# An attention stage reordered: next step's first scores beside this step's second scores, output product ahead of the gates

## The chip, the cores and the metric

The kernel runs on one core of a Trainium2 chip. Its time is the device time of one launch in microseconds; the number given is the median of several runs.

## What is computed

Sixteen sequences of 256 tokens with 256 features pass through a mixture-of-experts layer, an attention layer with 16 heads, the experts again, and a closing part (look-up-table FFN, gated recurrence, FFN). The change touches the attention layer alone. Cut to what matters:

```
q = x @ Wq ; k = x @ Wk ; v = x @ Wv ; s = clip(x @ Ws, -32, 32)      # x: normalised stream, per head 64, 64, 128, 64 wide
z = cumlogsumexp(s) ; p = exp(s - z) ; g = exp(z[t-1] - z[t])          # 64 slots a head
hk[t] = hk[t-1] * g[t] + k[t] p[t]^T ; ok[t] = q[t] @ hk[t]            # first read: a score for each slot
pv = softmax(ok)
hv[t] = hv[t-1] * g[t] + p[t] v[t]^T ; ov[t] = pv[t] @ hv[t]           # second read: over the slots
o = rmsnorm(ov) * g_norm * silu(x @ Wg) ; out = x + o @ Wo
```

The kernel has no recurrence. Since `p` and `g` are ratios of running sums of exp(s), the first read is a causal product (scores q k^T, masked, times exp(s), divided by the running sum), and the second is another (scores of the divided softmax weights with exp(s), masked, times v).

## The kernel before

`attention` (from line 803) works in N = 64 steps: 16 sequences of 4 quads of heads (HQ = 4, QPB = 4), T = 256 tokens as TT = 2 tiles of 128, heads in NH = 2 pairs. Each engine has a list of its own written out by hand; semaphores (`wait_ge`, `then_inc`) tie them. An engine runs its list strictly in order, so a wait holds all that stands behind it. Step n works on quad n while projections and first scores of quad n+1 are made ahead.

TensorE's list in a step is the loop at the end of the function: `value(n+1,0)`, `slots_read(n)` (first read: masked scores `at` times exps, into bank psC[0], semaphore `ok_ps`), `state_of_slots(n)` (sum over the first tile, psB[0]), `slots(n+1)` (projection for s), `turn_back(n)` (transposes of `okn`, the divided first read; waits `okn_ok`), `value(n+1,1)`, `query(n+1)`, `turn_weights(n)`, `turn_exps(n+1)`, `turn_output(n-1)`, `key(n+1)`, `scores_b(n)` (second scores, own 128x128 blocks only, psB), `state_read(n)` (psD), `gate(n+1,0)`, every fourth step `turn_stream`, `gate(n+1,1)`, `over_j(n)` (masked second scores times v, psD), `output(n-1)` (product with Wo, psC[0]) and `scores_a(n+1)` (first scores, four heads, each in a bank of its own: a 256-column and a 128-column matmul). The contraction of scores and state reads is 64 rows, so heads of the two parities stand in different halves of the array. Projections and `output` split each factor in a high and a low part and take three products (`split_matmul`, lines 1488 to 1490).

VectorE (DVE) in a step: `okn(n)` (line 1170), `clip(n+1)`, maximum, subtraction and sum of the softmax, `pzT` (1188), `low_of_output(n-1)`, `masked_second(n)` (1123), `running_sum` twice (1140), `invert` twice (reciprocal, 1144), `gated_output(n,1)` and `(n,0)` (1133), `gate(n+1,0)` and `(n+1,1)` (1129), `add_output(n-1)` (1107), `masked_first(n+1)` (1117, four parts of 384 columns), `squares(n)` (1148, 1151). ScalarE (ACT) copies out of PSUM (line 989), takes exp (1011, 1052), the squares (1067) and the gate's tanh (1027), in the order of its own loop. GpSimd (POOL) makes the root of the norm (978), scales the output (983) and, between, a table look-up.

PSUM has eight banks: psA and psB and psC two each, psD two. Reuse of a bank is what many waits are for.

Of the kernel before, what the change touches and what calls it, by code (L numbers as in the profile page):

```python
# [21 lines left out]
P = 128  # L22
# [780 lines left out]
def attention(nc, cst, w, tag, past, stream_a, stream_b, x_out, second, zero_row, indices, looked_up):  # L803
# [10 lines left out]
    with ExitStack() as ctx:  # L814
# [16 lines left out]
        at = mem.sb("at", [P, HQ, 3 * P])  # L831
        bt = at.rearrange("p h i -> p (h i)")[:, 0:HQ * T].rearrange("p (q s i) -> p q s i", q=2, i=P)
        state = at.rearrange("p h i -> p (h i)")[:, HQ * T:HQ * T + NH * DV].rearrange("p (a v) -> p a v", a=NH)
        sq = mem.sb("sq", [P, TT * HQ * DV])
        okn = sq[:, 0:NH * T].rearrange("p (a t) -> p a t", a=NH)
# [18 lines left out]
        psO = [psD[:, k, :] for k in range(2)]  # L854
        first_banks = psB + [psC[1], psO[0]]
# [4 lines left out]
                 "at_ps at_ok ok_ps st_ps st_ok okn_ok okb_ps mx_ok sub_ok pe_ok sm_ok es_ok ezt_ps pzt_ok bt_ps bt_ok "  # L860
# [4 lines left out]
         at_ps, at_ok, ok_ps, st_ps, st_ok, okn_ok, okb_ps, mx_ok, sub_ok, pe_ok, sm_ok, es_ok, ezt_ps, pzt_ok, bt_ps, bt_ok,  # L865
# [21 lines left out]
        with nc.Block(no_gpsimd_drain=True) as block:  # L887
# [99 lines left out]
            def _(act):  # L987
# [3 lines left out]
                def high_of_stream(b):  # L991
                    act.wait_ge(ln_ps, b + 1)
                    if b > 0:
                        act.wait_ge(g_ps, TT * QPB * b)
                    copy(lnT[:, 0, :, :].rearrange("p c t -> p (c t)"), psC[0], lnTh_ok)
# [26 lines left out]

                def gate_tanh(m, t):
                    if m > 0:
                        act.wait_ge(o1_ok, TT * m)
                    act.wait_ge(g_ps, TT * m + t + 1)
                    nc.scalar.activation(tg[:, t, :], psA[(1 - m % 2) if t == 0 else m % 2], ACT.Tanh, scale=0.5).then_inc(th_ok, 1)
# [11 lines left out]
                key(0)  # L1039
                turned_exps(0)  # L1040
                gate_tanh(0, 0)
                gate_tanh(0, 1)
                for n in range(N):
# [13 lines left out]
                    if ahead:  # L1057
                        key(n + 1)
                        turned_exps(n + 1)
                        if (n + 1) % QPB == QPB - 1 and n + 2 < N:  # L1060
                            high_of_stream((n + 1) // QPB + 1)
                    for p in range(2):
                        if p == 0:
                            act.wait_ge(ov_ps, 2 * n + 1)
# [3 lines left out]
                    if ahead:  # L1068
                        gate_tanh(n + 1, 0)
                        gate_tanh(n + 1, 1)  # L1070
                high_of_output(N - 1)

            @block.vector
            def _(dve):
# [14 lines left out]
                def low_of_stream(b):  # L1089
                    dve.wait_ge(lnTh_ok, b + 1)  # L1090
                    nc.vector.tensor_tensor(out=lnT[:, 1, :, :].rearrange("p c t -> p (c t)"), in0=psC[0],
# [21 lines left out]

                def masked_first(m):
                    for h in range(HQ):
                        dve.wait_ge(at_ps, HQ * m + h + 1)
                        nc.vector.tensor_tensor(out=at[:, h, :], in0=first_banks[h][:, 0:3 * P],
                                                in1=cst["causal"][:, :, :].rearrange("p a i -> p (a i)"), op=ALU.mult).then_inc(at_ok, 1)

                def masked_second(n):  # L1120
                    for p in range(2):
                        dve.wait_ge(bt_ps, 2 * n + p + 1)
                        nc.vector.tensor_tensor(out=bt[:, p, :, :], in0=psB[p].rearrange("p (s i) -> p s i", i=P),  # L1123
                                                in1=cst["causal"][:, 0, :].unsqueeze(1).to_broadcast([P, HQ, P]), op=ALU.mult).then_inc(bt_ok, 1)
# [35 lines left out]
                for a in range(NH):  # L1160
                    invert(0, a)
                gate(0, 0)
                gate(0, 1)
                masked_first(0)
                for n in range(N):
# [26 lines left out]
                    if ahead:  # L1192
                        dve.wait_ge(pzt_ok, n + 1)
                        running_sum(n + 1, 0)
                        running_sum(n + 1, 1)
                        invert(n + 1, 0)
                        if (n + 1) % QPB == QPB - 1 and n + 2 < N:
                            low_of_stream((n + 1) // QPB + 1)
                        invert(n + 1, 1)
                    dve.wait_ge(ov_ps, 2 * n + 2)  # L1200
# [7 lines left out]
                    if n > 0:  # L1208
                        add_output(n - 1)
                    if ahead:  # L1210
                        masked_first(n + 1)
# [5 lines left out]
            def _(pe):  # L1217
                ident = cst["ident"][:, :]

                def turn_stream(b):  # L1220
                    pe.wait_ge(ln_ok, TT * b + TT)
                    if b > 0:
                        pe.wait_ge(pzt_ok, QPB * b - 1)
                    for t in range(TT):
                        for c in range(DC):
                            mm = nc.tensor.transpose(psC[0][:, c * T + t * P:c * T + (t + 1) * P], ln[:, t, c * P:(c + 1) * P], ident)
# [45 lines left out]
                def gate(m, t):  # L1272
                    if t == 0:
                        pe.wait_ge(q_ok, m + 1)
                    else:
                        pe.wait_ge(k_ok, m + 1)
# [8 lines left out]

                def scores_a(m):
# [830 lines left out]
```

## Time and profile before

| | us |
|---|---|
| median of 3 runs | 2667.67 (2666.32 to 2668.74) |
| the profiled execution's own time | 2663.76 |
| its span, first to last instruction | 2662.0 |
| TensorE matmul busy | 2339.8 |
| VectorE busy | 1749.2 |
| ScalarE busy | 887.0 |
| GpSimd busy | 1238.2 |

The page cuts the span into 40 slices of 66.6 us; its digits are tenths of a slice that an engine was busy, or of full speed that TensorE's clock was granted. Attention takes the slices from about the sixth to the 27th. Busy times of overlapping matmuls are not their cost: that is read from start to start. "Idle before" behind an instruction is how long its engine stood, with what released it.

### The profile page before, as it was taken

What the parts mean: (1) busy time and instruction counts of PE and PEld (TensorE: products, weight loads), DVE (VectorE), ACT (ScalarE), POOL (GpSimd) and SP (SyncE); (2) the same over time, 40 slices, a digit from 0 to 9 for tenths busy, and PEclk for the clock granted to TensorE, in tenths of its full rate; (3) what the DMA queues carried; (4) which work ended last, traced back from release to release, by engine and by line L of the source; (5) the groups of instructions that cost most, each with busy time, mean ns of one, the idle gap of its engine ahead of it and who ended that gap; (6) DMA issues with size and microseconds to landing.
All of it is one profiled execution on the core that took longest, in us unless ns stands there. A gap on an engine that the chain in (4) does not pass through costs nothing. (4 is left out here: it accounts for less than half of the span.)

```text
span 2662.0 us, 45792 instructions
## 1 busy us (share of the span) xinstructions
PE 2339.8 (88%) x17782; PEld 2078.3 (78%) x17782; DVE 1749.2 (66%) x3450; ACT 887.0 (33%) x1768; POOL 1238.2 (47%) x1214
## 2 busy tenths in 40 slices
PE   7556499999999999999999999987566489999998
PEld 6444379999999999999999999976455377888887
DVE  6433267877787778777877887766422266776654
ACT  4323233333333333333333333324322133333332
POOL 3377735555555555545554555452378512222111
PEclk9698999999999999999999999998698798999999
DMA  7999700000000000000000000006699600000000
GB/s 241 291 222 225 145 13 9 17 17 21 5 21 17 21 5 17 21 21 5 17 21 21 6 17 21 13 3 175 178 231 215 137 20 21 25 24 25 14 12 16
DMA packets 196934, 169.60 MB, mean 64 GB/s; under 512 B 28945, under 2 KB 189681, under 8 KB 196209
## 3 DMA queue, kind: packets, MB, share of 16 engines
q1 hardware_dynamic: 168144, 123.94, 15.6%
q0 software_dynamic: 24576, 37.77, 7.8%
q10 hardware_dynamic: 4000, 4.98, 0.6%
q8 instruction: 143, 2.34, 0.4%
q14 instruction: 71, 0.57, 0.1%
HBM read 117.94 MB, written 53.13 MB: 64 GB/s over the span
## 5 line engine op out<-in xcount | busy, mean ns | idle before, releaser
L978 POOL TENSOR_TENSOR a_orstd<-a_ms,minus_half 128x8 f32<-128x8 f32 x64 | 106.7, 1667 | 466.3 <-DVE a_ms L1151 466.3
L958 POOL TENSOR_SCALAR a_pick<-a_index,lut_row 128x258 f32<-128x258 int32 x240 | 280.8, 1170 | 24.3
L1144 DVE RECIPROCAL a_rz<-a_rz 128x256 f32<-128x256 f32 x128 | 215.6, 1716 | 0.0
L777 DVE TENSOR_TENSOR e_hT<-e_psH,e_sil 128x128 f32<-128x128 f32 x128 | 37.2, 291 | 263.2 <-ACT e_sil L735 263.1
L661 PE MATMUL e_psX<-ident,e_xg 128*128 128x128 f32 x256 | 61.1, 325 | 166.8 <-DMA e_xg<-rows,slot_tok 166.6
L661 PEld LDWEIGHTS e_psX<-ident,e_xg 128*128 128x128 f32 x256 | 31.6, 156 | 209.7 <-DMA e_xg<-rows,slot_tok 205.4
L961 POOL TENSOR_TENSOR a_found<-a_found,a_pick 128x258 f32<-128x258 f32 x240 | 177.2, 738 | 20.0
L631 POOL DMA_INDIRECT e_xg<-rows,slot_tok x128 | 128.3, 1002 | 108.2 <-POOLq L253 69.8
L989 ACT ACTIVATE a_v<-a_psA 128x512 f32<-128x512 f32 x128 | 76.6, 598 | 229.5 <-PE a_psA L1490 229.5
L1488 PE MATMUL a_psC<-wo_high,a_oT 128*128 128x256 f32 x512 | 150.5, 294 | 1.5 <-DVE a_oT L1097 1.5
L1488 PE MATMUL f_pair<-f_lnT,wguT 128*128 128x512 f32 (+1 forms) x352 | 143.5, 408 | 7.5 <-DVE f_lnT L1754 7.2
L1489 PE MATMUL a_psC<-wo_low,a_oT 128*128 128x256 f32 x512 | 144.7, 283 | 0.0
L1490 PE MATMUL a_psC<-wo_high,a_oT 128*128 128x256 f32 x512 | 144.7, 283 | 0.0
L1765 DVE TENSOR_TENSOR f_hs<-f_pair,f_sil 128x512 f32<-128x512 f32 x96 | 66.0, 689 | 116.7 <-PE f_pair L1490 106.5
L1490 PE MATMUL f_pair<-f_lnT,wguT 128*128 128x512 f32 (+1 forms) x352 | 140.8, 400 | 0.0
L1489 PE MATMUL f_pair<-f_lnT,wguT 128*128 128x512 f32 (+1 forms) x352 | 140.7, 400 | 0.0
L983 POOL TENSOR_TENSOR a_o<-a_o,a_orstd 128x512 f32<-128x512 f32 x128 | 131.0, 1044 | 5.0
L1067 ACT ACTIVATE a_sq<-a_psD 128x512 f32<-128x512 f32 x128 | 76.5, 598 | 164.2 <-DVE a_o L1133 98.1
L1371 PEld LDWEIGHTS a_psD<-a_v,a_at 128*128 128x128 f32 x1024 | 124.1, 191 | 5.7
L1662 ACT ACTIVATE f_sil<-f_pair 128x512 f32<-128x512 f32 x96 | 57.2, 597 | 210.6 <-PE f_pair L1490 210.6
L719 ACT ACTIVATE e_xgT<-e_psX 128x256 f32<-128x256 f32 x128 | 49.1, 383 | 229.9 <-PE e_psX L661 225.8
L1123 DVE TENSOR_TENSOR a_at<-a_psB,causal 128x512 f32<-128x512 f32 x128 | 82.4, 686 | 64.5 <-PE a_psB L1320 64.5
(263 smaller groups left out, 7825.8 us busy)
## 6 DMA issues: line engine op xcount, KB each, us to landing
e_wg<-in_L_ffn_w_gate SPq DMA_DIRECT2D x128, 128.0 KB, 3.3
e_wu<-in_L_ffn_w_up SPq DMA_DIRECT2D x128, 128.0 KB, 3.7
e_wd<-in_L_ffn_w_down SPq DMA_DIRECT2D x128, 128.0 KB, 4.1
rows<-r_row SPq DMA_DIRECT2D x32, 320.0 KB, 3.3
stream_b<-r_zeros SPq DMA_DIRECT2D x11, 384.0 KB
stream_c<-rows SPq DMA_DIRECT2D x33, 128.0 KB, 3.2
r_xt<-in_L_attn_hidden_states SPq DMA_DIRECT2D x16, 256.0 KB, 5.8
stream_a<-r_xt SPq DMA_DIRECT2D x16, 256.0 KB, 4.3
```

The source lines that it names most:

```text
L631: pool.indirect_dma_start(out=xg[:, e % U, :], out_offset=None, in_=rows, in_offset=bass.IndirectOffsetOnAxis(ap=slot_tok[:, e:e + 1], axi ...
L661: nc.tensor.transpose(psX[u][:, c, :], xg[:, e % U, c * P:(c + 1) * P], cst["ident"][:, :]).then_inc(turned[u], 1)
L958: nc.gpsimd.tensor_scalar(pick[:, :, :], index[:, :, :], float(c), w["lut"][:, c:c + 1], ALU.is_equal, ALU.mult).then_inc(picked, 1)
L961: nc.gpsimd.tensor_tensor(out=found[:, :, :], in0=found[:, :, :], in1=pick[:, :, :], op=ALU.add).then_inc(looked, 1)
L978: nc.gpsimd.tensor_tensor(out=flat(orstd[:, :, :]), in0=ms[:, :], in1=cst["minus_half"][:, 0:TT * HQ], op=ALU.pow).then_inc(orstd_ok, 1)
L983: nc.gpsimd.tensor_tensor(out=part, in0=part, in1=orstd[:, :, 2 * a:2 * a + 2].unsqueeze(3).to_broadcast([P, TT, 2, DV]), op=ALU.mult).the ...
L1123: nc.vector.tensor_tensor(out=bt[:, p, :, :], in0=psB[p].rearrange("p (s i) -> p s i", i=P), in1=cst["causal"][:, 0, :].unsqueeze(1).to_br ...
L1144: nc.vector.reciprocal(rz[:, a, :], rz[:, a, :]).then_inc(rz_ok, 1)
L1371: mm = nc.tensor.matmul(psD[:, p, (t * NH + a) * DV:(t * NH + a + 1) * DV], bt[:, p, a * TT + t, :], v[:, n % 2, t, h * DV:(h + 1) * DV], ...
L1488: nc.tensor.matmul(out, lhs[0], rhs[0], start=first, stop=False)
L1489: nc.tensor.matmul(out, lhs[0], rhs[1], start=False, stop=False)
L1490: return nc.tensor.matmul(out, lhs[1], rhs[0], start=False, stop=last)
```

## The change

The first scores lose their own banks and shape. `own_scores` now makes the 128x128 diagonal blocks of either score product (first or second), two banks with four blocks each: for the first scores in psA, for the second in psB as before. The lower blocks (queries of the second tile, keys of the first) go by `scores_below` to the first half of psD's two banks, which ACT copies to a new tile `below` without a mask. DVE masks the diagonal blocks in two operations (`masked`) instead of four.

In TensorE's list `scores_a(n+1)` and `scores_below(n+1)` stand between `scores_b(n)` and `state_read(n)`; `output(n-1)` and `over_j(n)` follow, and then the gates, which now wait for the masks (`at_ok`), since they reuse psA. `value(n+1,0)` stands behind `state_of_slots(n)`. `over_j` waits for `below_ok` and signals once (`ov_ps`) instead of per parity. In DVE's list `masked_first(n+1)` follows `masked_second(n)`, `add_output(n-1)` is ahead of the gated outputs, and the two `invert` and `low_of_stream` are behind the gates, ahead of `squares(n)`. In ACT's list `below_copy` is ahead of `turned_exps`, and `high_of_stream` behind the tanhs. `turn_stream` uses psB[1] instead of psC[0]. `bt` moves from the tile of `at` into that of `sq`.

```diff
--- before.py
+++ after.py
...
@@ -1019,6 +1018,11 @@
                 def state_copy(n):
                     act.wait_ge(st_ps, n + 1)
                     copy(flat(state), psS, st_ok)
+
+                def below_copy(m):
+                    act.wait_ge(below_ps, m + 1)
+                    for p in range(2):
+                        copy(flat(below[:, p, :, :]), psD[:, p, 0:NH * P], below_ok)
 
                 def gate_tanh(m, t):
                     if m > 0:
@@ -1037,6 +1041,7 @@
                 value(0, 1)
                 query(0)
                 key(0)
+                below_copy(0)
                 turned_exps(0)
                 gate_tanh(0, 0)
                 gate_tanh(0, 1)
@@ -1056,18 +1061,19 @@
                         high_of_output(n - 1)
                     if ahead:
                         key(n + 1)
+                        below_copy(n + 1)
                         turned_exps(n + 1)
-                        if (n + 1) % QPB == QPB - 1 and n + 2 < N:
-                            high_of_stream((n + 1) // QPB + 1)
                     for p in range(2):
                         if p == 0:
-                            act.wait_ge(ov_ps, 2 * n + 1)
+                            act.wait_ge(ov_ps, n + 1)
                         else:
                             act.wait_ge(o1_ok, 2 * n + 1)
                         nc.scalar.activation(of_parity(p, sq), read_out(p), ACT.Square).then_inc(sq_ok, 1)
                     if ahead:
                         gate_tanh(n + 1, 0)
                         gate_tanh(n + 1, 1)
+                        if (n + 1) % QPB == QPB - 1 and n + 2 < N:
+                            high_of_stream((n + 1) // QPB + 1)
                 high_of_output(N - 1)
 
             @block.vector
...
@@ -1111,17 +1117,17 @@
                     dve.wait_ge(s_ps, m + 1)
                     nc.vector.tensor_scalar(flat(em[:, :, :]), psA[1 - m % 2], -32.0, 32.0, ALU.max, ALU.min).then_inc(sc_ok, 1)
 
+                def masked(out, banks, at, ready, done):
+                    for p in range(2):
+                        dve.wait_ge(ready, 2 * at + p + 1)
+                        nc.vector.tensor_tensor(out=out[:, p, :, :], in0=banks[p].rearrange("p (s i) -> p s i", i=P),
+                                                in1=cst["causal"][:, 0, :].unsqueeze(1).to_broadcast([P, HQ, P]), op=ALU.mult).then_inc(done, 1)
+
                 def masked_first(m):
-                    for h in range(HQ):
-                        dve.wait_ge(at_ps, HQ * m + h + 1)
-                        nc.vector.tensor_tensor(out=at[:, h, :], in0=first_banks[h][:, 0:3 * P],
-                                                in1=cst["causal"][:, :, :].rearrange("p a i -> p (a i)"), op=ALU.mult).then_inc(at_ok, 1)
+                    masked(at, [psA[1 - m % 2], psA[m % 2]], m, at_ps, at_ok)
 
                 def masked_second(n):
-                    for p in range(2):
-                        dve.wait_ge(bt_ps, 2 * n + p + 1)
-                        nc.vector.tensor_tensor(out=bt[:, p, :, :], in0=psB[p].rearrange("p (s i) -> p s i", i=P),
-                                                in1=cst["causal"][:, 0, :].unsqueeze(1).to_broadcast([P, HQ, P]), op=ALU.mult).then_inc(bt_ok, 1)
+                    masked(bt, psB, n, bt_ps, bt_ok)
 
                 def gate(m, t):
 
@@ -1159,9 +1165,9 @@
                     running_sum(0, a)
                 for a in range(NH):
                     invert(0, a)
+                masked_first(0)
                 gate(0, 0)
                 gate(0, 1)
-                masked_first(0)
                 for n in range(N):
                     b, q = divmod(n, QPB)
                     ahead = n + 1 < N
@@ -1190,14 +1196,13 @@
                         low_of_output(n - 1)
                     masked_second(n)
                     if ahead:
+                        masked_first(n + 1)
                         dve.wait_ge(pzt_ok, n + 1)
                         running_sum(n + 1, 0)
                         running_sum(n + 1, 1)
-                        invert(n + 1, 0)
-                        if (n + 1) % QPB == QPB - 1 and n + 2 < N:
-                            low_of_stream((n + 1) // QPB + 1)
-                        invert(n + 1, 1)
-                    dve.wait_ge(ov_ps, 2 * n + 2)
+                    if n > 0:
+                        add_output(n - 1)
+                    dve.wait_ge(ov_ps, n + 1)
                     dve.wait_ge(tg_ok, TT * n + TT)
                     gated_output(n, 1)
                     dve.wait_ge(sq_ok, 2 * n + 1)
@@ -1205,10 +1210,10 @@
                     if ahead:
                         gate(n + 1, 0)
                         gate(n + 1, 1)
-                    if n > 0:
-                        add_output(n - 1)
-                    if ahead:
-                        masked_first(n + 1)
+                        if (n + 1) % QPB == QPB - 1 and n + 2 < N:
+                            low_of_stream((n + 1) // QPB + 1)
+                        invert(n + 1, 0)
+                        invert(n + 1, 1)
                     squares(n)
                 low_of_output(N - 1)
                 add_output(N - 1)
@@ -1220,10 +1225,10 @@
                 def turn_stream(b):
                     pe.wait_ge(ln_ok, TT * b + TT)
                     if b > 0:
-                        pe.wait_ge(pzt_ok, QPB * b - 1)
+                        pe.wait_ge(bt_ok, 2 * (QPB * b - 1))
                     for t in range(TT):
                         for c in range(DC):
-                            mm = nc.tensor.transpose(psC[0][:, c * T + t * P:c * T + (t + 1) * P], ln[:, t, c * P:(c + 1) * P], ident)
+                            mm = nc.tensor.transpose(psB[1][:, c * T + t * P:c * T + (t + 1) * P], ln[:, t, c * P:(c + 1) * P], ident)
                     mm.then_inc(ln_ps, 1)
 
                 def project(name, dst, m, t, width, ready):
@@ -1270,10 +1275,7 @@
                     project_turned("k", psA[m % 2], m, k_ps)
 
                 def gate(m, t):
-                    if t == 0:
-                        pe.wait_ge(q_ok, m + 1)
-                    else:
-                        pe.wait_ge(k_ok, m + 1)
+                    pe.wait_ge(at_ok, 2 * m + t + 1)
                     project("g", psA[(1 - m % 2) if t == 0 else m % 2], m, t, HQ * DV, g_ps)
 
                 def turn_exps(m):
@@ -1283,21 +1285,33 @@
                             mm = nc.tensor.transpose(psC[1][:, a * T + t * P:a * T + (t + 1) * P], em[:, t, a * P:(a + 1) * P], ident)
                     mm.then_inc(et_ps, 1)
 
+                def own_scores(lhs, rhs, banks, ready):
+
+                    for a in range(NH):
+                        for t in range(TT):
+                            for p in range(2):
+                                r, own = p * DK, slice(t * P, (t + 1) * P)
+                                mm = nc.tensor.matmul(banks[p][:, (a * TT + t) * P:(a * TT + t + 1) * P], lhs[r:r + DK, a, own], rhs[r:r + DK, a, own],
+                                                      start=True, stop=True)
+                                if a == NH - 1 and t == TT - 1:
+                                    mm.then_inc(ready, 1)
+
                 def scores_a(m):
 
                     pe.wait_ge(k_ok, m + 1)
                     pe.wait_ge(q_ok, m + 1)
-                    pe.wait_ge(et_ok, m + 1)
-                    if m > 0:
-                        pe.wait_ge(bt_ok, 2 * m)
-                    for h in range(HQ):
-                        if h == 3 and m > 0:
-                            pe.wait_ge(o1_ok, TT * m)
-                            pe.wait_ge(sq_ok, TT * m)
-                        bank, a, r = first_banks[h], h // 2, (h % 2) * DK
-                        nc.tensor.matmul(bank[:, 0:2 * P], kT[r:r + DK, a, 0:P], qT[r:r + DK, a, 0:T], start=True, stop=True)
-                        nc.tensor.matmul(bank[:, 2 * P:3 * P], kT[r:r + DK, a, P:T], qT[r:r + DK, a, P:T],
-                                         start=True, stop=True).then_inc(at_ps, 1)
+                    own_scores(kT, qT, [psA[1 - m % 2], psA[m % 2]], at_ps)
+
+                def scores_below(m):
+
+                    if m > 1:
+                        pe.wait_ge(otl_ok, NH * (m - 1))
+                    for a in range(NH):
+                        for p in range(2):
+                            r = p * DK
+                            mm = nc.tensor.matmul(psD[:, p, a * P:(a + 1) * P], kT[r:r + DK, a, 0:P], qT[r:r + DK, a, P:T], start=True, stop=True)
+                    if m == 0:
+                        mm.then_inc(below_ps, 1)
 
                 def state_of_slots(n):
 
@@ -1313,36 +1327,34 @@
                     pe.wait_ge(pzt_ok, n + 1)
                     pe.wait_ge(et_ok, n + 1)
                     pe.wait_ge(st_ok, n + 1)
-                    for a in range(NH):
-                        for t in range(TT):
-                            for p in range(2):
-                                r, own = p * M, slice(t * P, (t + 1) * P)
-                                mm = nc.tensor.matmul(psB[p][:, (a * TT + t) * P:(a * TT + t + 1) * P], emT[r:r + M, a, own], pzT[r:r + M, a, own],
-                                                      start=True, stop=True)
-                                if a == NH - 1 and t == TT - 1:
-                                    mm.then_inc(bt_ps, 1)
-
-                def state_read(n):
+                    pe.wait_ge(lnTl_ok, n // QPB + 1)
+                    own_scores(emT, pzT, psB, bt_ps)
+
+                def state_read(n, more):
 
                     if n > 0:
                         pe.wait_ge(otl_ok, NH * n)
                     for a in range(NH):
                         for p in range(2):
                             r = p * M
-                            nc.tensor.matmul(psD[:, p, (NH + a) * DV:(NH + a + 1) * DV], pzT[r:r + M, a, P:T], state[r:r + M, a, :],
-                                             start=(a == 0), stop=False, skip_group_check=True)
+                            mm = nc.tensor.matmul(psD[:, p, (NH + a) * DV:(NH + a + 1) * DV], pzT[r:r + M, a, P:T], state[r:r + M, a, :],
+                                                  start=(a == 0), stop=False, skip_group_check=True)
+                    if more:
+                        mm.then_inc(below_ps, 1)
 
                 def slots_read(n):
 
                     if n > 1:
                         pe.wait_ge(acc_ok, n - 1)
+                    pe.wait_ge(at_ok, 2 * n + 2)
+                    pe.wait_ge(below_ok, 2 * n + 2)
                     for a in range(NH):
-                        pe.wait_ge(at_ok, HQ * n + 2 * a + 2)
-                        for i, (t, j) in enumerate(((0, 0), (1, 0), (1, 1))):
-                            for h in (2 * a, 2 * a + 1):
-                                r = (h % 2) * M
+                        for t, j in ((0, 0), (1, 0), (1, 1)):
+                            for p in range(2):
+                                h, r = 2 * a + p, p * M
+                                scores = at[:, p, a * TT + t, :] if t == j else below[:, p, a, :]
                                 mm = nc.tensor.matmul(psC[0][r:r + M, a * T + t * P:a * T + (t + 1) * P], em[:, j, h * M:(h + 1) * M],
-                                                      at[:, h, i * P:(i + 1) * P], start=(j == 0), stop=(j == t))
+                                                      scores, start=(j == 0), stop=(j == t))
                     mm.then_inc(ok_ps, 1)
 
                 def turn_back(n):
@@ -1363,6 +1375,8 @@
 
                 def over_j(n):
 
+                    if n + 1 < N:
+                        pe.wait_ge(below_ok, 2 * n + 4)
                     for p in range(2):
                         pe.wait_ge(bt_ok, 2 * n + p + 1)
                         for a in range(NH):
@@ -1370,7 +1384,7 @@
                                 h = 2 * a + p
                                 mm = nc.tensor.matmul(psD[:, p, (t * NH + a) * DV:(t * NH + a + 1) * DV], bt[:, p, a * TT + t, :],
                                                       v[:, n % 2, t, h * DV:(h + 1) * DV], start=False, stop=True, skip_group_check=True)
-                        mm.then_inc(ov_ps, 1)
+                    mm.then_inc(ov_ps, 1)
 
                 def turn_output(n):
                     for a in range(NH):
@@ -1397,16 +1411,16 @@
                 query(0)
                 key(0)
                 turn_exps(0)
+                scores_a(0)
+                scores_below(0)
                 gate(0, 0)
                 gate(0, 1)
-                scores_a(0)
                 for n in range(N):
                     ahead = n + 1 < N
-                    if ahead:
-                        value(n + 1, 0)
                     slots_read(n)
                     state_of_slots(n)
                     if ahead:
+                        value(n + 1, 0)
                         slots(n + 1)
                     turn_back(n)
                     if ahead:
@@ -1420,18 +1434,18 @@
                     if ahead:
                         key(n + 1)
                     scores_b(n)
-                    state_read(n)
+                    if ahead:
+                        scores_a(n + 1)
+                        scores_below(n + 1)
+                    state_read(n, ahead)
+                    if n > 0:
+                        output(n - 1)
+                    over_j(n)
                     if ahead:
                         gate(n + 1, 0)
                         if (n + 1) % QPB == QPB - 1 and n + 2 < N:
                             turn_stream((n + 1) // QPB + 1)
                         gate(n + 1, 1)
-                    over_j(n)
-                    if n > 0:
-                        pe.wait_ge(lnTl_ok, min((n + 1) // QPB + (2 if (n + 1) % QPB == QPB - 1 else 1), B))
-                        output(n - 1)
-                    if ahead:
-                        scores_a(n + 1)
                 turn_output(N - 1)
                 pe.wait_ge(acc_ok, N - 1)
                 output(N - 1)
```

## Rows read from the trace of the kernel before

**Rows 1.** the page, section 2: 40 slices of the span

```profile
PE   7556499999999999999999999987566489999998
PEclk9698999999999999999999999998698798999999
```

**Rows 2.** stretches (begin:end, length, busy PE, PEld, DVE, ACT, POOL, clock, DMA)

```profile
1002.44:1024.77 22.33, 22.33 (x193) 20.25 (x192) 18.09 (x31) 7.89 (x15) 14.14 (x15) 1.00 0.15 48
```

**Rows 3.** timeline of PE, one step (start, us, engine, line, out<-in, count)

```profile
1002.24 0.28 PE L1490 MATMUL a_psC<-wo_high,a_oT 128*128 128x256 f32 x1
1002.45 0.71 PE L1298 MATMUL a_psB<-a_qT,a_kT 64*128 64x256 f32 x4
1004.05 0.50 PE L1488 MATMUL a_psA<-wv_high,a_lnT 128*128 128x512 f32 x1
...
1005.32 0.39 PE L1490 MATMUL a_psA<-wv_high,a_lnT 128*128 128x512 f32 x1
1005.64 1.53 PE L1344 MATMUL a_psC<-a_at,a_em 128*64 128x128 f32 x24
...
1007.54 0.39 PE L1488 MATMUL a_psA<-ws_high,a_lnT 128*128 128x256 f32 x1
...
1008.96 0.28 PE L1490 MATMUL a_psA<-ws_high,a_lnT 128*128 128x256 f32 x1
1009.08 0.38 PE L1353 MATMUL a_psC<-ident,a_sq 128*128 128x128 f32 x2
```

**Rows 4.** timeline of PE, later in this step

```profile
1015.61 1.16 PE L1320 MATMUL a_psB<-a_pzT,a_emT 64*128 64x128 f32 x16
1016.60 0.61 PE L1332 MATMUL a_psD<-a_at,a_pzT 64*128 64x128 f32 x8
...
1019.81 0.39 PE L1490 MATMUL a_psA<-wg_high,a_lnT 128*128 128x512 f32 x1
```

**Rows 5.** timeline of DVE, around this step

```profile
1001.99 1.28 DVE L1129 SCALAR_TENSOR_TENSOR a_tg<-a_tg,a_psA 128x512 f32<-128x512 f32 x2 [0.67 <-ACT a_tg L1027]
1003.19 0.68 DVE L1107 TENSOR_TENSOR a_xacc<-a_psC,a_xacc 128x512 f32<-128x512 f32 x1
...
1019.17 3.34 DVE L1144 RECIPROCAL a_rz<-a_rz 128x256 f32<-128x256 f32 x2
1022.43 1.22 DVE L1133 TENSOR_TENSOR a_o<-a_psD,a_tg 128x512 f32<-128x512 f32 x2
```

**Rows 6.** timelines of PE (10.68) and ACT, in this step

```profile
1010.68 0.39 PE L1490 MATMUL a_psA<-wv_high,a_lnT 128*128 128x512 f32 x1
...
1001.36 1.09 ACT L1027 ACTIVATE a_tg<-a_psA 128x512 f32<-128x512 f32 x2
...
1011.11 0.60 ACT L989 ACTIVATE a_v<-a_psA 128x512 f32<-128x512 f32 x1 [0.48 <-PE a_psA L1490]
...
1015.71 0.60 ACT L989 ACTIVATE a_kT<-a_psA 128x512 f32<-128x512 f32 x1 [0.78 <-PE a_psA L1490]
```

**Rows 7.** timelines of DVE and PE, last step

```profile
1770.40 1.21 DVE L1148 TENSOR_REDUCE a_ss<-a_sq 128x8 f32<-128x1024 f32 x1
...
1771.73 0.69 DVE L1170 TENSOR_TENSOR a_sq<-a_psC,a_rz 128x512 f32<-128x512 f32 x1
1772.47 0.66 PE L1353 MATMUL a_psC<-ident,a_sq 128*128 128x128 f32 x4 [0.62 <-DVE a_sq L1170]
```

**Rows 8.** timeline of PE in the expert stages, two waits

```profile
263.47 0.44 PE L661 MATMUL e_psX<-ident,e_xg 128*128 128x128 f32 x2 [2.47 <-DMA e_xg<-rows,slot_tok]
...
1960.68 0.44 PE L661 MATMUL e_psX<-ident,e_xg 128*128 128x128 f32 x2 [2.28 <-DMA e_xg<-rows,slot_tok]
```

**Rows 9.** stretches and PE's waits in the expert stages

```profile
262.00:316.00 54.00, 30.27 (x204) 23.41 (x204) 18.53 (x39) 14.98 (x37) 43.35 (x33) 1.00 0.81 176
1961.30:1964.70 3.40, 3.40 (x17) 3.11 (x16) 0.77 (x2) 1.27 (x4) 2.79 (x3) 0.51 0.66 144
PE e_psX L661 <- DMA e_xg<-rows,slot_tok: 24.0, 16, 2.5
```

More of the change, by code:

```diff
@@ L830, in attention @@
         rz = mem.sb("rz", [P, NH, T])
-        at = mem.sb("at", [P, HQ, 3 * P])
-        bt = at.rearrange("p h i -> p (h i)")[:, 0:HQ * T].rearrange("p (q s i) -> p q s i", q=2, i=P)
-        state = at.rearrange("p h i -> p (h i)")[:, HQ * T:HQ * T + NH * DV].rearrange("p (a v) -> p a v", a=NH)
+        at = mem.sb("at", [P, 2, HQ, P])
+        below = mem.sb("below", [P, 2, NH, P])
+        state = below[:, 0, :, :]
         sq = mem.sb("sq", [P, TT * HQ * DV])
+        bt = sq.rearrange("p (q s i) -> p q s i", q=2, i=P)
         okn = sq[:, 0:NH * T].rearrange("p (a t) -> p a t", a=NH)
@@ L853, in attention @@
         psD = mem.ps("psD", [P, 2, 512])
-        psO = [psD[:, k, :] for k in range(2)]
-        first_banks = psB + [psC[1], psO[0]]
         psS = psB[0][:, 0:NH * DV]
@@ L859, in attention @@
                  "v_ps v_ok q_ps q_ok k_ps k_ok g_ps th_ok tg_ok s_ps sc_ok em_ok scan_ok rz_ok et_ps et_ok "
-                 "at_ps at_ok ok_ps st_ps st_ok okn_ok okb_ps mx_ok sub_ok pe_ok sm_ok es_ok ezt_ps pzt_ok bt_ps bt_ok "
+                 "at_ps at_ok below_ps below_ok ok_ps st_ps st_ok okn_ok okb_ps mx_ok sub_ok pe_ok sm_ok es_ok ezt_ps pzt_ok bt_ps bt_ok "
                  "ov_ps sq_ok ss_ok ms_ok orstd_ok o1_ok o2_ok ot_ps oth_ok otl_ok out_ps acc_ok "
@@ L864, in attention @@
          v_ps, v_ok, q_ps, q_ok, k_ps, k_ok, g_ps, th_ok, tg_ok, s_ps, sc_ok, em_ok, scan_ok, rz_ok, et_ps, et_ok,
-         at_ps, at_ok, ok_ps, st_ps, st_ok, okn_ok, okb_ps, mx_ok, sub_ok, pe_ok, sm_ok, es_ok, ezt_ps, pzt_ok, bt_ps, bt_ok,
+         at_ps, at_ok, below_ps, below_ok, ok_ps, st_ps, st_ok, okn_ok, okb_ps, mx_ok, sub_ok, pe_ok, sm_ok, es_ok, ezt_ps, pzt_ok, bt_ps, bt_ok,
          ov_ps, sq_ok, ss_ok, ms_ok, orstd_ok, o1_ok, o2_ok, ot_ps, oth_ok, otl_ok, out_ps, acc_ok,
@@ L994, in high_of_stream @@
                         act.wait_ge(g_ps, TT * QPB * b)
-                    copy(lnT[:, 0, :, :].rearrange("p c t -> p (c t)"), psC[0], lnTh_ok)
+                    copy(lnT[:, 0, :, :].rearrange("p c t -> p (c t)"), psB[1], lnTh_ok)
                 def value(m, t):
@@ L1090, in low_of_stream @@
                     dve.wait_ge(lnTh_ok, b + 1)
-                    nc.vector.tensor_tensor(out=lnT[:, 1, :, :].rearrange("p c t -> p (c t)"), in0=psC[0],
+                    nc.vector.tensor_tensor(out=lnT[:, 1, :, :].rearrange("p c t -> p (c t)"), in0=psB[1],
                                             in1=lnT[:, 0, :, :].rearrange("p c t -> p (c t)"), op=ALU.subtract).then_inc(lnTl_ok, 1)
```

## The prediction

> **What bounds the kernel now.** I read the page's slices first: TensorE is at 99% with a full clock from about 340 to 1770 us, the attention stage, and nothing outside that stage is touched by the change [rows 1]. Then one stretch: in a step of 22.33 us PE is busy throughout, VectorE (DVE) for 18.1, ScalarE (ACT) for 7.9 [rows 2]. A busy PE may still be waiting with overlapped ends, so I read PE's timeline next, by the starts of its matmuls. One step of the 64 takes 22.33 us (it begins with `scores_a` at 1002.45, the next at 1024.77 [rows 2, 3]), and every section follows the one before at 0.09 to 0.2 us above its normal spacing. PE is the bound, with no wait that costs more than a change of shape. DVE is idle for 4.2 us of the step [rows 2]. So the change can win only by making PE's list shorter, and loses where a new order makes PE wait for the slack engine. I therefore cost first the list, then each wait.
>
> **PE's own list.** Starts, not durations, are added here, since matmuls overlap.
> - Removed: the shape change after the output product (2.24 to 2.45 against a spacing of 0.12: 0.09), `scores_a` alone (2.45 to 4.05: 1.60), `value(n+1,0)` after it (4.05 to 5.64: 1.59), `slots` as the first 128-row section after `state_of_slots` (7.54 to 9.08: 1.54) [rows 3]. Sum 4.82.
> - Added: own and lower blocks as 12 pairs of 64-row matmuls, 2 passes each. `scores_b` has the same form: 16 passes in 8 pairs take 0.99 with the start-up, and the 8 passes of `state_read` go on behind it [rows 4]; that is 0.109 a pair once started, so 12 x 0.109 = 1.31 with no start-up, between `scores_b` and `state_read`. `slots_read` behind the gates costs 0.32 from the last matmul (5.32 to 5.64 [rows 3]) in place of the plain spacing of a 512-column matmul, 0.23 (4.05 to 5.32 is five of them and 0.1 of start-up): 0.09. `value(n+1,0)` now starts the 128-row section: 6 x 0.233 + 0.11 = 1.51. `slots` behind it has no start-up (7.54 to 8.96 is eleven spacings and 0.11, so 0.119 each): 12 x 0.118 = 1.42. Sum 4.33.
> - So PE's list falls by 0.49, from 22.33 to 21.84 us. Over the 63 steps that make a next one: -31 us. `output` and `over_j` change places with the gates at no cost: the same kinds of neighbours.
>
> Here a rule speaks against the change. The Trainium skill, "TensorE: Matmul & The Clock Gate", section "LDWEIGHTS (loading the stationary operand)", says that a weight load takes its columns at 1.2 GHz, so about 107 ns for 128. The blocks need 24 loads where 16 stood; were the 8 more not hidden, they would cost an estimated 0.85 us a step, 54 us in all, and PE's list would grow by 0.36. I go by the row of `scores_b`, where 16 such loads fit into 0.99 us.
>
> **Edits with no price.** DVE masks two whole banks in place of four parts (two 128x512 operations, about 0.6 apart as the gates are [rows 5]) right behind the second mask; the gates' new wait for it is met while PE still has `output` and `over_j` to do. The two `below_copy` on ACT stand between `state_read` and `over_j`, with `output` (24 x 0.12 = 2.9 us) as cover; two copies at most as long as a 512-column one are 1.2 [rows 6], and without the cover `over_j` would wait that long. `scores_a` needs the copied keys: the key copy runs from 15.71 to 16.31 [rows 6], and `scores_b` ends at 16.60 [rows 4], so it is there 0.3 early; bounds are 0 and 0.3, I take 0 by these rows. `add_output` and the single `ov_ps` add no lateness: both are ahead of the gates. The moved `turn_stream` costs PE the same; SP's queue and POOL's list have no step moved.
>
> **The wait that is added.** Behind the gates, DVE now does gate 0, gate 1, both `invert`, `squares(n)`, and only then `okn(n+1)`, the product that `turn_back(n+1)` on PE waits for. Before, the two inversions ran under the gates' matmuls, and PE had `over_j`, `output`, `scores_a` and `value` to do meanwhile. Both sides of the race, from the start of the last gate matmul:
> - DVE's side. The `tanh` starts 0.43 behind the last 512-column matmul (the value copy: 10.68 to 11.11 [rows 6]). Gate 1 starts 0.63 after its tanh (1001.36 to 1001.99 [rows 5, 6]); the inversions start 0.61 later (half of 1.99 to 3.19), and the two take 3.26 (19.17 to 22.43) [rows 5]. `squares` to `okn` takes 1.33, and `okn` to the first matmul of `turn_back` 0.74: the last step already shows this, since DVE is late there, and PE stands 0.62 us for it [rows 7]. Sum 0.43 + 0.63 + 0.61 + 3.26 + 1.33 + 0.74 = 7.00 us.
> - PE's side, without waiting: 0.32 to `slots_read`, 1.90 for it and `state_of_slots` (5.64 to 7.54 [rows 3]), 1.51, 1.42: 5.15 us.
> - So `turn_back` waits 1.85 us, in every step from 1 to 63. Everything behind it on PE (`value(n+1,1)`, query, weights, key, scores, output, `over_j`, gates) is in the same queue, and the next race starts only when the gates end, so nothing catches up. The period is 21.84 + 1.85 = 23.69. DVE's other idle time lies in front of `add_output` and of the gated outputs, ahead of the gates, where it helps nothing.
> The term has bounds of 1.55 and 2.15 (0.05 less or more at each of six hand-overs, an estimate from one of them: 0.63 from start to start, 0.67 by its idle time [rows 5]). I take 1.85, the sum of the rows.
>
> In 15 steps a stream is turned between the gates, and its `low_of_stream` now stands ahead of the inversions: 0.6 us more each, 9 us. At the end `output(62)` no longer covers the tail of `over_j(63)`: about 3 us.
>
> **The clock.** A step gets an idle stretch on PE of 1.85 less 0.16 of the last matmul's tail, 1.7 us, and about 2.3 in the 15. After an idle stretch of 2.28 us the granted clock was 0.51 for the next 3.4 us; after one of 2.47 it stayed full, and in 54 us with 16 waits of 1.5 on average (24.0 in all) it stayed 1.00 [rows 8, 9]. I take none for the 1.7 and half of the 15, 7 x 1.7 (half of 3.4 us of work lost) = 12 us.
>
> **Sum.** -31 + 63 x 1.85 (117) + 9 + 3 + 12 = +110 us. Against the profiled execution's own 2663.8 us this is 2774; the median of the runs shown stands 3.9 us above it, so 2778.
>
> **Rivals.**
> - The low clock spreads (12%). If the stall is rather 2.15 or more, many of the 63 are followed by a low stretch at 1.7 to 3.4 us each: -31 + 135 + 9 + 3, and 25 x 2.2 = 55: +171, 2839. For it: the 2.28 us row [rows 8]. Against: the 16 waits of 1.5, of which the longest was 2.5.
> - DVE keeps up and the kernel is faster (8%). DVE is idle for 4.2 us of a step [rows 2], and masks less than before. If the chain behind the gates were at most 5.15 us, `turn_back` would find `okn` done: only -31 + 3 + 0 is left, 2640. It decides at a chain of 5.15; for that the inversions would have to run ahead of gate 1. The order in DVE's list forbids it, and the last step shows that `okn` really stands behind `squares`.
> - In between (7%): a chain of 5.6 to 6.4 us, a stall of 0.5 to 1.2, and with it 2681 to 2725.
> - The 8 additional loads are not hidden (3%). Each would then cost at most one more spacing of a pair, 0.109 [rows 4]: 0.87 us a step, 55 in all, 2833. The section of the Trainium skill named above bears on this.
> - The likeliest (70%): 2778, alone from 2747 to 2809 by the bounds of the stall and of the clock.
>
> Range: 2738 to 2832 leaves out the faster rival, half of the low-clock one and some of the middle. A difference under 0.2% (5 us) is about what a measurement of this kernel can't tell from none. Faster by more: 8%; within: 2%; slower: 90%.
>
> **What the profile after would show.** PE: an idle stretch of 1.7 us ahead of `turn_back` in each step, put down to DVE's `a_sq` product, with no `over_j` or score wait. DVE: no idle time from gate 1 to `okn`, the inversions behind the gates; idle ahead of `add_output` and the gated outputs. A period near 23.7 us. Twelve score pairs at 0.109 between `scores_b` and `state_read`. The prediction is wrong if `turn_back` follows `slots` at once, if `scores_a` waits for the key copy, if `over_j` waits for ACT's copies, or if the clock's row shows falls in the attention stage beyond a few.

## The result and the profile after

| | before | after |
|---|---|---|
| median of 4 runs, us | 2666.99 | 2777.66 (2775.72 to 2780.87) |
| ratio, 95% interval | | 1.0416 (1.0404 to 1.0429) |
| profiled execution, span | 2662.0 | 2774.7 |
| attention, first to last matmul | 1462.2 | 1571.0 |
| a plain step, `turn_back` to `turn_back`, median | 22.33 | 23.77 |

The changed kernel is 4.2% slower. Of the 112.7 us in the span, 108.8 lie between the first and the last attention matmul, and 3.9 outside. A plain step is one without the turned stream between its gates; the 15 with it are called stream steps below. The page's slices (now 69.4 us each), which answer to [rows 1], look alike: attention is as full and its clock digits are as high, so the loss is not to be seen in this view:

```profile
PE   6556489999999999999999999996566568999998
PEclk9688899999999999999999999997789979999999
```

One step as a stretch (columns as in [rows 2]). PE, busy for all of 22.33 us before, is now idle for 1.7 of 23.80, while VectorE is busy for 16.9:

```profile
1020.21:1044.01 23.80, 22.09 (x204) 20.10 (x202) 16.89 (x24) 8.55 (x16) 10.06 (x10) 1.00 0.06 12
```

TensorE in this step, which answers to [rows 3, 4]. The gate's last matmul is at 1029.40, `value` follows `state_of_slots` at 1031.63, and after the last of `slots` (1034.45) the engine stands until 1036.43. Below, `scores_b`, the own blocks, the lower blocks and `state_read` run in one go, the 24 passes of the new scores from 1044.01 to 1045.35:

```profile
1029.40 0.40 PE L1504 MATMUL a_psA<-wg_high,a_lnT 128*128 128x512 f32 x1
1029.73 0.44 PE L1356 MATMUL a_psC<-a_at,a_em 128*64 128x128 f32 x4
...
1031.63 0.50 PE L1502 MATMUL a_psA<-wv_high,a_lnT 128*128 128x512 f32 x1
...
1034.45 0.28 PE L1504 MATMUL a_psA<-ws_high,a_lnT 128*128 128x256 f32 x1
1036.43 0.66 PE L1365 MATMUL a_psC<-ident,a_sq 128*128 128x128 f32 x4 [1.70 <-DVE a_sq L1176]
...
1043.01 1.16 PE L1294 MATMUL a_psB<-a_pzT,a_emT 64*128 64x128 f32 x16
1044.01 1.06 PE L1294 MATMUL a_psA<-a_qT,a_kT 64*128 64x128 f32 x16
1044.90 0.61 PE L1312 MATMUL a_psD<-a_qT,a_kT 64*128 64x128 f32 x8
1045.35 0.61 PE L1340 MATMUL a_psD<-a_below,a_pzT 64*128 64x128 f32 x8
1045.89 0.39 PE L1502 MATMUL a_psC<-wo_high,a_oT 128*128 128x256 f32 x1
```

ScalarE's second tanh and VectorE behind the gates, which answer to [rows 5 to 7]. No gap is left between gate 1 and the product `a_sq<-a_psC,a_rz` (that is `okn`), which ends the wait:

```profile
1029.89 0.60 ACT L1031 ACTIVATE a_tg<-a_psA 128x512 f32<-128x512 f32 x1 [0.80 <-PE a_psA L1504]
```

```profile
1030.53 0.69 DVE L1135 SCALAR_TENSOR_TENSOR a_tg<-a_tg,a_psA 128x512 f32<-128x512 f32 x1 [0.71 <-ACT a_tg L1031]
1031.13 3.36 DVE L1150 RECIPROCAL a_rz<-a_rz 128x256 f32<-128x256 f32 x2
1034.40 1.16 DVE L1154 TENSOR_REDUCE a_ss<-a_sq 128x8 f32<-128x1024 f32 x1
...
1035.68 0.69 DVE L1176 TENSOR_TENSOR a_sq<-a_psC,a_rz 128x512 f32<-128x512 f32 x1
```

TensorE's largest wait in attention, from 400 to 1800 us (total, times, longest):

```profile
PE a_psC L1365 <- DVE a_sq L1176: 104.5, 58, 2.1
```

One wait for the masks is there too, once, before the first step. There no `output` and no `over_j` stand between the scores and the first gate, and on VectorE the masks stand behind both inversions, so TensorE is idle for 3.30 us:

```profile
349.90 3.34 DVE L1150 RECIPROCAL a_rz<-a_rz 128x256 f32<-128x256 f32 x2
353.16 1.22 DVE L1123 TENSOR_TENSOR a_at<-a_psA,causal 128x512 f32<-128x512 f32 x2
```

```profile
353.84 0.79 PE L1502 MATMUL a_psA<-wg_high,a_lnT 128*128 128x512 f32 x1 [3.30 <-DVE a_at L1123]
```

### The profile page after: what moved, and what is told of

It is laid out like the page before. It is cut to its first block and busy times, and to the rows that moved or that the text cites. A ratio compares the mean times of both kernels' runs of the same rounds, so it can differ in the third digit from the quotient of the medians.

```text
span 2774.7 us, 46756 instructions
## 1 busy us (share of the span) xinstructions
PE 2331.5 (84%) x18294; PEld 2072.2 (75%) x18294; DVE 1730.7 (62%) x3322; ACT 927.9 (33%) x1896; POOL 1237.2 (45%) x1214
## 5 line engine op out<-in xcount | busy, mean ns | idle before, releaser
L1135 DVE SCALAR_TENSOR_TENSOR a_tg<-a_tg,a_psA 128x512 f32<-128x512 f32 x128 | 88.0, 687 | 104.1 <-ACT a_tg L1031 104.1
L1365 PE MATMUL a_psC<-ident,a_sq 128*128 128x128 f32 x256 | 42.4, 289 | 116.0 <-DVE a_sq L1176 116.0
L1139 DVE TENSOR_TENSOR a_o<-a_psD,a_tg 128x512 f32<-128x512 f32 x128 | 84.7, 691 | 69.8 <-PE a_psD L1385 69.8
```

The costliest lines, as they stand in the source:

```text
L1135: nc.vector.scalar_tensor_tensor(out=tg[:, t, :], in0=tg[:, t, :], scalar=1.0, in1=psA[(1 - m % 2) if t == 0 else m % 2], op0=ALU.add, op1 ...
L1139: nc.vector.tensor_tensor(out=of_parity(p, flat(o1[:, :, :])), in0=read_out(p), in1=of_parity(p, flat(tg[:, :, :])), op=ALU.mult).then_inc ...
```

## Experiments

All times are medians; the ratio is to the kernel before, run beside it on the same chip (e1, e2, e4 and e7 on one chip, e3, e5 and e6 on another, e8 and e9 on a third). "Period" is the median from one `turn_back` to the next; "gap" is the time from the start of the matmul ahead of `turn_back` to its own, 0.12 us where nothing is waited for. A row that begins with PEld counts the idle time of the weight loads, which is somewhat longer than the delay from start to start. The theory was that the time is lost in a race behind the gates: VectorE's chain up to `okn` against the TensorE work up to `turn_back`. Such a race has a bend: as long as VectorE's side is the shorter one, its length costs nothing; beyond that, each microsecond costs one.

**e1_inverts_ahead.**

```diff
                         running_sum(n + 1, 1)
+                        invert(n + 1, 0)
+                        invert(n + 1, 1)
                     if n > 0:
                         add_output(n - 1)
...
                         gate(n + 1, 1)
...
-                        invert(n + 1, 0)
-                        invert(n + 1, 1)
```

> The changed kernel with one edit in VectorE's list: both inversions stand right behind the running sums, ahead of the output addition, instead of behind the gates. Theory (the wait is a race behind the gates): the chain from the last gate matmul to the first matmul of turn_back falls from 7.03 to 3.8 us, against 5.2 us of TensorE work; no wait at turn_back, a period of 21.9 us, about 2644 us. Rival 1 (the new score blocks and the new order on TensorE cost the time themselves): the period stays near 23.8 and the time within 10 us of 2778. Rival 2 (the inversions are only moved to another late place: VectorE comes 0.9 us late to the gated outputs, and tanh, gates and squares pass it on): a wait of 0.9 us stays, about 2700.

2644.4 us, ratio 0.9911 (0.9895 to 0.9928), period 21.87. The whole loss goes, and a gain stays. VectorE is in fact late for the output addition and the gated outputs, but both end in time:

```profile
1012.46 3.34 DVE L1150 RECIPROCAL a_rz<-a_rz 128x256 f32<-128x256 f32 x2
1015.72 0.63 DVE L1113 TENSOR_TENSOR a_xacc<-a_psC,a_xacc 128x512 f32<-128x512 f32 x1
1016.26 1.28 DVE L1139 TENSOR_TENSOR a_o<-a_psD,a_tg 128x512 f32<-128x512 f32 x2
1018.20 1.49 DVE L1135 SCALAR_TENSOR_TENSOR a_tg<-a_tg,a_psA 128x512 f32<-128x512 f32 x2 [0.67 <-ACT a_tg L1031]
1019.61 1.21 DVE L1154 TENSOR_REDUCE a_ss<-a_sq 128x8 f32<-128x1024 f32 x1
...
1020.94 0.68 DVE L1176 TENSOR_TENSOR a_sq<-a_psC,a_rz 128x512 f32<-128x512 f32 x1
```

`okn` would allow `turn_back` from 1021.68, and TensorE comes to it at 1023.04, at its plain spacing:

```profile
1022.93 0.28 PE L1504 MATMUL a_psA<-ws_high,a_lnT 128*128 128x256 f32 x1
1023.04 0.49 PE L1365 MATMUL a_psC<-ident,a_sq 128*128 128x128 f32 x3
```

Both rivals fall: the new order on TensorE costs nothing by itself, and VectorE's lateness is not passed on. This is also the fastest kernel of the study, 0.9% ahead of the one before and 4.8% ahead of the changed one.

**e2_one_ahead.** Only `invert(n + 1, 0)` is moved ahead.

> The changed kernel with one of the two inversions moved ahead of the output addition, the other left behind the gates. Theory: the chain is 7.03 less 1.65 = 5.4 us against 5.2, so 0.2 us of wait is left and all but a tenth of it is gone: about 2656. Rival (each inversion takes its own share, half of the wait stays): 0.93 us a step, about 2710.

2670.4 us, ratio 1.0009 (0.9997 to 1.0021), period 22.18. The direction and the bend are the theory's: of 1.86 us of wait 0.25 is left, not half. The size was missed by 14 us, in my own count. The plain steps lose 0.3 to e1 and not 0.2; the 15 stream steps lose 0.62 each (23.19 against 22.57), because `low_of_stream` stands behind the gates too, and I had left them out; the last interval and the tail behind it are 2.6 longer together. The wait and the one for the turned stream, from 400 to 1700 us:

```profile
PEld a_psC L1365 <- DVE a_sq L1176: 22.8, 58, 0.7
...
PEld a_psA L1502 <- DVE a_lnT L1097: 6.2, 15, 0.4
```

**e3_one_between.** One inversion ahead, the other between the two gates.

> The changed kernel with one inversion ahead of the output addition and the other between the two gates, where VectorE stands 1.15 us for the second tanh. Theory: the chain from the last gate matmul is 0.5 us of gate 1's delay longer than with both ahead, still under 5.2: no wait at turn_back, the time of e1_inverts_ahead within 3 us, and low_of_stream keeps its place. Rival (the second gate's delay is passed on whole, 1.65 us): a wait of 0.3 us, 20 us above e1_inverts_ahead.

2651.3 us, ratio 0.9937 (0.9916 to 0.9957), period 21.87 as in e1: no wait at `turn_back`. It is 7 us over e1 and not within 3, though part of that may lie between two chips: between the first and the last attention matmul the traces differ by 5.0. These are not where the rival had them either, in each step, but in the 15 stream steps (22.92 against 22.57): the delayed gate delays `low_of_stream`, and `value` of the next sequence waits for it, 0.77 us a time against 0.41 in e1. First e3, then e1:

```profile
PEld a_psA L1502 <- DVE a_lnT L1097: 11.5, 15, 0.8
```

```profile
PEld a_psA L1502 <- DVE a_lnT L1097: 6.2, 15, 0.4
```

**e7_half_sum.** The sum of squares reads half of each head's values, so half of the norm's sum is left out.

```diff
-                    nc.vector.reduce_sum(ss[:, :], sq.rearrange("p (s v) -> p s v", v=DV), axis=AX.X).then_inc(ss_ok, 1)
+                    nc.vector.reduce_sum(ss[:, :], sq.rearrange("p (s v) -> p s v", v=DV)[:, :, 0:DV // 2], axis=AX.X).then_inc(ss_ok, 1)
```

> The changed kernel, its sum of squares taken over half of each head's 128 values: the reduction reads 512 columns instead of 1024, and half of the norm's sum is left out. Nothing is moved. Theory (all that VectorE does behind the gates is in the race): the chain is 0.5 us shorter, the wait 1.35 instead of 1.86, 33 us less, and a few low clock stretches less: about 2742. Rival (only the inversions count, since the squares have slack of their own): 2778.

2739.2 us, ratio 1.0265 (1.0247 to 1.0282), period 23.26. The gap before `turn_back` falls from 1.98 to 1.44 us, which is 34 us in all, and the four low-clock stretches of the changed kernel's stream steps are gone, some 6 more; 38 were measured. What is saved in an operation that was not moved comes off the wait in full too: the race is over everything behind the gates, not over the inversions. TensorE's wait from 400 to 1700 us:

```profile
PE a_psC L1365 <- DVE a_sq L1176: 69.7, 55, 1.5
```

**e4_extra_op.** One idle operation more behind the inversions.

```diff
...
+                        if n > 0:
+                            dve.wait_ge(idled, n)
+                        nc.vector.reduce_max(idle[:, :], cst["causal"][:, :, :], axis=AX.X).then_inc(idled, 1)
                     squares(n)
```

> The changed kernel with one more VectorE operation behind the inversions in each step, a maximum over 384 constant columns, some 0.4 us, whose result nothing reads. Theory: the wait grows by the operation's whole duration, 0.4 x 63 = 26 us, to 2804; idle stretches of 2.1 us on TensorE in plain steps are then as long as the ones of the 15 stream steps are now, of which 5 were followed by a low clock, so about a third of the 63 steps is followed by one, 16 more at 1.55 us: 25 us, about 2829. Rival (the low clock needs a longer idle stretch than that and came by another cause): 2804 with no more low stretches than now.

2834.0 us, ratio 1.0619 (1.0602 to 1.0637). The gap before `turn_back` is 2.43 us, 0.45 longer, and a plain step 24.25; that is 28 us of the 56 over the changed kernel. The rest is the clock. In the attention stage it fell 22 times next to a `turn_back`, against 5 times in the changed kernel, and a step with such a fall is 1.55 us longer: 17 more are 26 us. Clock digits of the page, and the wait from 400 to 1700 us:

```profile
PEclk9788799999999999999999999997878979999999
```

```profile
PE a_psC L1369 <- DVE a_sq L1177: 116.7, 52, 2.5
```

**e5_scores_alone.** The new blocks between `scores_b` and `state_read`; gates, `over_j` and `output` in the order of before; `value(n+1,0)` ahead of `slots_read`; on VectorE the inversions (with `low_of_stream` between them) behind the running sums, and the output addition behind the gates.

> The scores' part of the change alone: own and lower blocks between scores_b and state_read, but gates, over_j and output in the order of the kernel before, value ahead of slots_read, and VectorE's inversions ahead of the gated outputs, as before. Theory (the new blocks save 0.42 us of TensorE's list a step, as the changed kernel's period of 23.77 less 1.86 of wait shows; the gates now wait about 0.3 us for the masks, which four operations of 0.6 us behind scores_b give): a period of 22.2, about 2660. Rival (the 8 more weight loads eat the gain): at least 2667, with scores_b and the blocks at more than 0.12 us a pair.

2689.4 us, ratio 1.0079 (1.0062 to 1.0096), period 22.37. Slower than I expected by 29 us, though not by the rival's mechanism: the pairs run at 0.11 us. Read from the waits, the blocks' saving is spent on VectorE. The first gate stands for the masked product in each step (first line): it starts 0.46 us behind the last of `state_read`, against 0.20 in the kernel before, so 0.26 late. `value(n+1,0)` starts another 0.17 late behind `output` (0.29 against 0.12); in its list it waits for the first gate's product, though the profile names no releaser (second line). The saving without the neighbouring `value` and `slots` is 0.09 + 1.60 - 1.31 = 0.38, so 22.33 - 0.38 + 0.26 + 0.17 = 22.38 for a plain step, which is even with before. In the stream steps, 23.9 us against 23.0, `value` of the next sequence stands 1.1 us for the gate (third line), which I read as the gate and the turned stream standing behind four masks on VectorE; no run takes that apart. The lead-in adds 4 us, with the 3.3 us wait for the first masks that the changed kernel has too:

```profile
PEld a_psA L1503 <- DVE a_at L1123: 21.5, 57, 0.4
```

```profile
1019.99 0.19 PEld L1503 LDWEIGHTS a_psA<-wv_high,a_lnT 128*128 128x128 f32 x1 [0.18 <-issue]
```

```profile
PE a_psA L1503 <- DVE a_tg L1135: 15.4, 14, 1.4
```

**e6_over_j_first.** e1 with `over_j` ahead of `output`, and `add_output` behind the gated outputs.

> Kernel e1_inverts_ahead with over_j ahead of output on TensorE, and the output addition behind the gated outputs on VectorE. Theory (output is the cover of ACT's two copies and of the second mask): over_j waits about 0.9 us in each step, so 57 us above e1: about 2700. Rival (the copies and masks are early anyway): the time of e1, 2644.

2694.4 us, ratio 1.0094 (1.0075 to 1.0114), period 22.75, 0.87 above e1, as the theory had it: without `output` as cover, `over_j` stands for ACT's copies of the lower blocks, in 57 steps of 57:

```profile
PEld a_psD L1385 <- ACT a_below L988: 54.1, 57, 0.9
```

**e8_slack_two and e9_slack_five.** e1 with two and with five of the idle operations behind the gates, for the bend of the race.

> Kernel e1_inverts_ahead with two of e4's idle VectorE operations (0.45 us each from start to start) behind the gates. In e1's trace okn would let turn_back start at 1021.68 (1020.94 and 0.74) and it starts at 1023.05: 1.37 us of slack. Theory (a race with a bend): 0.9 us more stays under the slack, so plain steps cost nothing, and the 15 stream steps, where 0.6 of slack is used already, at most 0.15 each: the time of e1, 2644, within 4 us. Rival (the wait is proportional to what VectorE does behind the gates, with no bend): 0.9 x 63 = 57 us more, 2701.

2648.3 us, ratio 0.9921 (0.9904 to 0.9938): two are free, as e1's slack of 1.37 us says.

> Kernel e1_inverts_ahead with five of the idle operations, 2.25 us, behind the gates. Theory: 2.25 less 1.37 of slack is 0.88 us of wait in the plain steps and about 0.5 more in the 15 stream steps: 55 + 7 us above e1, about 2706. Rival (no bend): 2.25 x 63 = 142 us more, 2786.

2750.3 us, ratio 1.0304 (1.0286 to 1.0322), dearer than I expected by 44 us. The price of the operations was wrong, not the bend. In a row each waits for the one before, and the five take 2.81 us (16.52 to 19.33), not 2.25: they start 0.58 to 0.59 apart, and only behind the last, which nothing waits for, is it 0.47. 2.81 - 1.37 = 1.44 is just the wait that the trace has (a gap of 1.56 less the spacing of 0.12):

```profile
1016.52 2.90 DVE L1221 TENSOR_REDUCE a_idle<-causal 128x3 f32<-128x384 f32 x5
1019.33 1.21 DVE L1155 TENSOR_REDUCE a_ss<-a_sq 128x8 f32<-128x1024 f32 x1
```

```profile
PE a_psC L1370 <- DVE a_sq L1177: 76.3, 55, 1.6
```

## Why the prediction was right, point by point

The time came 0.3 us from the forecast. Its mechanism is shown; the last few microseconds of closeness are luck, since small terms missed both ways. In the profiled executions the change is 112.7 us where 110 were forecast: -29 from PE's list (forecast -31), 117 of wait (117), 3 of slower transposes (0), 5 in the stream steps (9), 6 of clock (12), 7 at the ends (3) and 4 outside the attention matmuls (0). The forecast then added 3.9 us to get from the profiled execution to the median; for the changed kernel this was 1.2.

- **PE's own list.** Forecast 21.84 us a step. e1, which has no wait, measures 21.87; the 8 more weight loads are hidden, as the row of `scores_b` had said: the 12 new pairs take 1.34 us (1044.01 to 1045.35), 0.112 each, where 1.31 was forecast. The rival of unhidden loads falls.
- **The race.** Chain forecast 7.00, measured 7.03 (1029.40 to 1036.43): tanh after 0.49, gate 1 after 0.64, inversions after 0.60, 3.27 for the two, 1.28 from `squares` to `okn`, 0.75 to `turn_back`. PE's side forecast 5.15, measured 5.17 (1029.40 to 1034.45, and 0.12). Wait 1.86 against 1.85. e1, e2, e7 and e9 move either side by known amounts and the wait follows.
- **A plain step.** Forecast 23.69, measured 23.77, 5 us in all. PE's list has 0.03 of it, and after a wait the four transposes of `turn_back` take 0.41 from their start to the next section's, against 0.35 in a running stream (all of e1, e3, e6 and the kernel before). The forecast had nothing for that.
- **The stream steps.** I put 0.6 on each for `low_of_stream`; they lose 1.77 (23.03 to 24.80) where a plain step loses 1.44 (22.33 to 23.77), so 0.33 more, because in them `value` already stands 0.24 for the turned stream, and that part of TensorE's list overlaps the longer chain. 5 us instead of 9.
- **The clock.** Forecast 7 falls in the 15, with idle stretches of about 2.3 us, and 12 us; the stretches measure 2.05, and 4 of the 15 were followed by a fall: 6 us. One more fall came at the last `turn_back`, so "5 of the 15" in what was expected of e4 is one too many. The rival of a spreading low clock, told by a stall of 2.15 or more, is just what e4 brings about with a stall of 2.31 (a gap of 2.43 less 0.12).
- **The ends.** Forecast 3. The lead-in to the first `turn_back` is 3.7 longer, the last interval 2.8 (a plain one 1.4), the tail 2.0: about 7 instead of 3. The lead-in is where an edit with no price had one: I had the gates' new wait for the masks met while PE does `output` and `over_j`, and before the first step it does neither. The first gate stands 3.30 us for it (353.84), and the clock is at half speed for the next 3.4 us, which it is not in the kernel before; a wait of 0.84 for the gates, which the kernel before has there, is gone.
- **The rivals.** That VectorE keeps up was put at 2640 with the condition that the inversions run ahead of gate 1. In the changed kernel they don't; e1 grants the condition and measures 2644.
- **Covers.** `below_copy` was put at nothing with `output` as cover and at most 1.2 without; e6 shows 0.87. That `scores_a` finds the keys copied holds (no such wait in the profile after). That the masks are ready for the gates holds only by the new place of `output` and `over_j`; e5 shows 0.26 without, and the first gate 3.30. So the two parts of the change need one another, and the third move, of the inversions, was what undid them.

## What to carry to other kernels

When work is moved ahead of a hand-over on the engine that is the bound, it also stops being cover for what stands behind that hand-over on the other engines: add up both sides of the race from the same instruction. An engine that is busy for 17 of 24 us can be the one that is waited for; its idle time helps only where its list has it. Here two lines moved in VectorE's list turn 4.2% slower into 0.9% faster.

## What the runs showed of the hardware

The granted clock of TensorE after idle stretches of known length, in one and the same surroundings, counted at the `turn_back` of each step: after 1.2 to 1.7 us none in 168 (e7, e9 and the changed kernel), after 2.0 to 2.2 us 14 in 64 (the changed kernel, e4 and one of e9), and after 2.4 to 2.5 us 12 in 16 (e4). Steps 0 and 63 are left out. Each fall was one low stretch of 3.4 us at half speed, which began between 0.3 us ahead of the `turn_back` and 1.5 us behind it, as this one (2.4 GHz before it, 1.2 GHz in it):

```profile
1012.40:1015.80 3.40, 3.40 (x15) 3.10 (x14) 1.63 (x4) 1.11 (x2) 3.22 (x4) 0.50 0.00 0
```

The length alone does not tell which stretch is followed by a fall: of those of 2.0 to 2.2 us 50 were not. In e4, 0.45 us more of wait a step, 28 us in all, therefore cost 56. I had expected half of the longer stretches of the changed kernel (2.1 us) to be followed by one; about a quarter is.
